# Convolution in blocks of 16 positions of one channel group, with tiles of one group of 16 rows

## The chip, the cores and the metric

The kernel runs on one core of one Trainium2 chip. The metric is the device time of one execution in microseconds (us). The core's engines are named as in the profile: PE (TensorE), DVE (VectorE), ACT (ScalarE), POOL (GpSimd) and SP (SyncE, which here only issues transfers). PE was granted a clock of 0.991 of full speed on average, which is its 2.4 GHz level almost throughout.

## What is computed

x is 128 x 32 x 512 (batch, channel, position), all float32. A grouped convolution over positions (4 groups of 8 channels, 9 taps, padding 4) plus a per-batch, per-channel condition is fed to a linear layer over the 512 positions with a routed LoRA; x is added to the result:

```python
out = lax.conv_general_dilated(x, weight, window_strides=(1,), padding=[(4, 4)],
        dimension_numbers=('NCH', 'OIH', 'NCH'), feature_group_count=4)
y = out + jnp.einsum('nd,od->no', c, c_weight)[:, :, None] + bias[None, :, None]
base_out = jnp.einsum('btd,od->bto', y, base_W) + base_b          # 512 -> 512
logits = jnp.einsum('btd,nd->btn', y, router_W) + router_b        # 512 -> 15
topk_p, topk_i = jax.lax.top_k(jax.nn.softmax(logits, -1), 8)
w = per-expert weight: topk_p summed by expert_map[topk_i]
h = jnp.einsum('btd,erd->bter', y, A)                             # 8 experts x 16
lora = jnp.einsum('bter,eor->bto', h * w[..., None], B) * 2.0
return x + base_out + lora
```

## The kernel before

Precision is kept by splitting each float32 operand into a high part (rounded by ACT) and a rest (the difference, made by DVE or POOL); every product is three matmuls: high by high, rest of the weights by high, high by rest of the data.

A tile is 128 rows of (batch, channel): 4 batches of 32 channels; there are 32 tiles, and the linear layer takes one tile per step. The convolution works in units of 16 channels (a half, h) of 8 batches, one unit per step, with blocks of 8 positions: partitions hold 8 positions x 16 channels. An output block needs two neighbouring input blocks. For even and odd blocks together this is done with three matrices: one for the block's own input, one for the reach into the next, and their sum. `terms` holds three operands of 256 columns: two differences of an even and an odd block (made by DVE, L672) and the odd block itself; so a unit is 3 x 3 = 9 matmuls of 256 columns (`conv`, L498). The sum of the shared product and the condition is made by DVE in `common` (L658), and added to both own products in one instruction of 512 columns that writes `y_rows` (L663). DVE turns `y_rows` into `y` by a block transposition (`turn`, L731), which needs both halves; ACT and POOL split it (`y_hi` L352, `y_lo` L443).

What an engine does in step t, in its own program order:
- PE (`step`): waits for `y_lo_ready` and `out_added`; 12 matmuls of 400 columns (the front bank: LoRA, router, half of the linear layer), then `front_done`; transposes `hw` of tile t-1 (`turn_hw`); 9 matmuls of 256; 6 of the LoRA's way up for tile t-1 (`up`, L540); 3 of 256; then `conv(t)`, which signals `common_done` after its first three matmuls and `conv_done` after the ninth.
- DVE: `condition` of the unit that PE made at the end of step t-1 (L658, L663), `turn(t+2)`, `difference` (L672 twice), `choose(t)` (L679, waits for `front_done`), `hw_low(t-1)`, `mark`, `weigh(t)` up to `hw` (L713), `add_out(t-1)` (L642, out of PSUM into `xr`), which signals `out_added`.
- ACT: `y_hi`, `hw_hi`, the exponentials, `terms_hi`, and a copy of the odd block to PSUM. POOL: `bias_rows` (L432), `y_lo`, `terms_lo` (L437). SP: stores and loads.

Steps 4 to 23 run in a loop of four steps each time round; 0 to 3 and 24 to 32 are written out. PSUM's two `wide_ps` sets alternate between tiles, so PE may begin step t only after `add_out(t-2)`, which is the last thing in DVE's step t-1. Before step 0 stands an opening that loads, splits and convolves the first tiles by ordinary products with two matrices; there POOL also adds the two convolution matrices (`conv_sum`).

## Time and profile before

| | |
|---|---|
| runs without the profiler | 197.27 us median of 3 (197.12, 197.27, 205.5) |
| the profiled execution's own time | 197.38 us |
| its span, first to last instruction | 195.6 us |
| busy: PE / DVE / POOL / ACT | 187.3 / 161.1 / 139.1 / 76.9 us |
| mean granted PE clock | 0.991 |
| bytes moved | 27.66 MB, 141 GB/s over the span |

The span is 1.8 us shorter than the time of the same execution. A row of the timeline gives the start and the duration; of DVE the duration of an instruction is longer than the distance to an independent next one. Matmuls are pipelined, so their durations overlap; the distance of two starts is what one costs on PE: 0.12 us for 256 columns, 0.18 us for 400. "idle before <-releaser" stands in brackets.

### The profile page before, as it was taken

To read this page: it belongs to the slowest core of one execution; us is meant where nothing else is said; L and a number is where in the kernel's file an instruction comes from. 1 tells how busy PE (TensorE), PEld (TensorE's weight loads), DVE (VectorE), ACT (ScalarE), POOL (GpSimd) and SP (SyncE) were. 2 spreads that over 40 slices of the span, in tenths; PEclk is the share of its full clock that TensorE was granted. 3 is DMA by queue.
4 is the path that set the end of the run, shared out by engine and by line. 5 is a ranking of instruction groups with operands and counts; after the bars stand their busy time and mean duration, and the time that the engine had idled before them with its cause. 6 is when DMAs were issued, how large, how long until landed. Compare 5 with 4: busy or idle time off the path is not lost.

```text
span 195.6 us, 4329 instructions
## 1 busy us (share of the span) xinstructions
PE 187.3 (96%) x1297; PEld 180.1 (92%) x1297; DVE 161.1 (82%) x547; ACT 76.9 (39%) x197; POOL 139.1 (71%) x115
## 2 busy tenths in 40 slices
PE   7899699999999999999999999999999999998993
PEld 2788599999999999999999999999999999997992
DVE  0899987888889888889888889888898889775663
ACT  3674434434333444433334444343344443122210
POOL 4539796777887777777887777778877777943520
PEclk9999969999999999999999999999999999999999
DMA  5985442455444434445443335444334133333312
GB/s 180 312 292 214 111 140 80 159 167 162 146 124 124 152 116 153 162 162 157 125 140 123 134 130 162 162 162 147 137 110 150 71 86 111 107 107 109 111 54 107
DMA packets 19051, 27.66 MB, mean 141 GB/s; under 512 B 2144, under 2 KB 9696, under 8 KB 19040
## 3 DMA queue, kind: packets, MB, share of 16 engines
q1 hardware_dynamic: 18576, 27.05, 42.6%
q10 hardware_dynamic: 432, 0.48, 0.7%
q8 instruction: 5, 0.08, 0.2%
q0 software_dynamic: 32, 0.01, 0.2%
q14 instruction: 6, 0.05, 0.1%
HBM read 19.14 MB, written 8.39 MB: 141 GB/s over the span
## 4 chain that ended last, share of the span: by engine, by line
PE 83%; DVE 8%; DMA 4%; issue 2%; ACT 1%; DVEq 0%; ACTq 0%
PE wide_ps L516 53%; PE conv_banks L498 15%; PE wide_ps L540 10%; DMA wide_sb<-wide_w 2%; DMA x_in<-x_first 2%; PE hwt_bank L527 2%; PE conv_banks L516 1%; DVE terms L672 1%; DVE y_rows L647 1%; DVE xr L642 1%; DVE wide_lo L757 1%; DVE y L731 1%; DVE spread L703 0%; DVE expert_w L707 0%; ACT wide_hi L324 0%
## 5 line engine op out<-in xcount | busy, mean ns | idle before, releaser
L516 PE MATMUL wide_ps<-wide_hi,y_hi 128*128 128x400 f32 (+1 forms) x248 | 80.4, 329 | 1.1 <-DVE xr L642 0.8
L516 PE MATMUL wide_ps<-wide_lo,y_hi 128*128 128x400 f32 (+1 forms) x248 | 77.1, 315 | 0.0
L516 PE MATMUL wide_ps<-wide_hi,y_lo 128*128 128x400 f32 (+1 forms) x248 | 76.8, 314 | 0.0
L437 POOL TENSOR_TENSOR terms_lo<-terms,terms_hi 128x768 fp32r<-128x768 f32 x28 | 51.6, 1842 | 31.8 <-ACT terms_hi L345 31.8
L516 PEld LDWEIGHTS wide_ps<-wide_hi,y_hi 128*128 128x128 f32 x248 | 46.6, 189 | 3.5 <-issue 1.0
L516 PEld LDWEIGHTS wide_ps<-wide_lo,y_hi 128*128 128x128 f32 x248 | 46.9, 190 | 0.0
L516 PEld LDWEIGHTS wide_ps<-wide_hi,y_lo 128*128 128x128 f32 x248 | 46.6, 189 | 0.0
L432 POOL TENSOR_TENSOR xr<-xr,biases_sb 128x512 f32<-128x512 f32 x32 | 41.3, 1291 | 5.6 <-DMA xr<-x_rows 5.5
L443 POOL TENSOR_TENSOR y_lo<-y,y_hi 128x512 fp32r<-128x512 f32 x31 | 40.2, 1295 | 3.3 <-ACT y_hi L352 3.3
L359 ACT ACTIVATE hw_hi<-hwt_bank 128x128 fp32r<-128x128 f32 x31 | 8.6, 277 | 81.7 <-PE hwt_bank L527 81.7
L352 ACT ACTIVATE y_hi<-y 128x512 fp32r<-128x512 f32 x32 | 20.2, 632 | 17.9 <-PE wide_ps L516 16.8
L345 ACT ACTIVATE terms_hi<-terms 128x768 fp32r<-128x768 f32 x28 | 23.2, 830 | 2.5 <-DVE terms L672 2.5
L498 PE MATMUL conv_banks<-terms_lo,conv_hi 128*128 128x256 f32 x84 | 24.0, 286 | 0.0
L498 PE MATMUL conv_banks<-terms_hi,conv_lo 128*128 128x256 f32 x84 | 24.0, 285 | 0.0
L498 PE MATMUL conv_banks<-terms_hi,conv_hi 128*128 128x256 f32 x84 | 23.9, 285 | 0.0
L731 DVE STREAM_TRANSPOSE y<-y_rows 128x512 f32<-128x512 f32 x32 | 22.6, 707 | 1.0
L663 DVE TENSOR_TENSOR y_rows<-conv_banks,common 128x512 f32<-128x512 f32 x28 | 19.4, 692 | 2.9
L642 DVE TENSOR_TENSOR xr<-wide_ps,xr 128x512 f32<-128x512 f32 x30 | 20.4, 682 | 0.5 <-PE wide_ps L540 0.3
L672 DVE TENSOR_TENSOR terms<-even,odd_bank 128x256 f32<-128x256 f32 x56 | 20.0, 395 | 0.0
L498 PEld LDWEIGHTS conv_banks<-terms_hi,conv_hi 128*128 128x128 f32 x84 | 16.0, 191 | 0.3 <-issue 0.3
L498 PEld LDWEIGHTS conv_banks<-terms_hi,conv_lo 128*128 128x128 f32 x84 | 16.1, 192 | 0.0
L498 PEld LDWEIGHTS conv_banks<-terms_lo,conv_hi 128*128 128x128 f32 x84 | 16.1, 191 | 0.0
...
## 6 DMA issues: line engine op xcount, KB each, us to landing
...
```

The lines of the kernel that those rows point to most:

```text
L345: nc.scalar.activation(terms_hi[i % 2][:, :, :, :], terms[i][:, :, :, :], ACT.Copy)\
L352: nc.scalar.activation(y_hi[k % 2][:, :, :], y[k % 2][:, :, :], ACT.Copy)\
L432: nc.gpsimd.tensor_tensor(xr[k][:, :], xr[k][:, :], base_b_sb[:, :], ALU.add)\
L437: nc.gpsimd.tensor_tensor(terms_lo[i % 2][:, :, :, :], terms[i][:, :, :, :], terms_hi[i % 2][:, :, :, :].bitcast(F32), ALU.subtract)\
L443: nc.gpsimd.tensor_tensor(y_lo[k % 2][:, :, :], y[k % 2][:, :, :], y_hi[k % 2][:, :, :].bitcast(F32), ALU.subtract)\
L498: mm = nc.tensor.matmul(sums, w[:, h, j, :], a[i][:, j, :, :], start=w is conv_hi and a is terms_hi, stop=a is terms_lo)
L516: mm = nc.tensor.matmul(sums_of(t, k)[:, b, 0:columns[1] - columns[0]], a[k % 2][:, r, :], w[:, r, columns[0]:columns[1]], start=r == 0 an ...
L540: mm = nc.tensor.matmul(sums_of(t, k)[:, b, first:first + HALF], a[k % 2][:, :], w[:, b * HALF:(b + 1) * HALF], start=False, stop=True, sk ...
L642: nc.vector.tensor_tensor(rows, linear_sums(t, k), rows, ALU.add)\
L663: nc.vector.tensor_tensor(y_rows[i][:, h, :, :].rearrange("p n (a k) -> p a n k", a=2), own_ps, common[:, :, :].unsqueeze(1).to_broadcast( ...
L672: d = nc.vector.tensor_tensor(terms[i][:, j, :, :], even[i][:, :, j:j + MK], odd_ps, ALU.subtract)
L731: nc.vector.transpose(y[k % 2][:, :, :].rearrange("p r (n h o) -> p h n r o", n=Q, h=HALVES), y_rows[(k // 2) % 2][:, :, own, :]).then_inc ...
```

## The change

Partitions now hold 16 positions x 8 channels: a unit is one channel group (of 4) of 16 batches, and a tile of the linear layer is that same unit, 128 rows of (batch, channel of the group). The input is brought into this order on the host (`x_units`, `x_edges`, `x_rows`), and the output back from it.

In blocks of 16 positions, an output block reaches into its neighbour with 8 positions only, half of the partitions; groups of even number reach forward, those of odd number backward, so that their reaching halves are different partitions. The products of the unit with its own and its sum matrix are 2 x 3 = 6 matmuls of 256 columns; the edges of two groups lie in one operand and one matrix (`edges`, `W_QUARTERS`, `edge_ps` in `hwt_bank`), 3 matmuls, made with the group of even number. So `conv` has 9 matmuls in odd steps and 6 in even steps. There is one difference per unit on DVE instead of two, and on POOL one edge difference and one `edge_lo` per two tiles; ACT has one `edge_hi` per two tiles; `terms_hi` and `terms_lo` have 512 columns instead of 768.

`condition` now waits for `conv_done` ahead of its first instruction, and has three instructions of 256 columns, each of which waits for the one before: shared product plus condition, own product plus that, and the edge product on 64 partitions. `turn(t)` needs only its own unit. `turn_hw(t-1)` of step t also waits until `condition(t+2)` is done, since the edge product is in the bank of its output. Fourteen matrices are loaded instead of four, in five pieces, and `conv_sum` is gone. In the opening the condition's weights and `expert_map` are loaded from ACT's queue behind the table load, POOL's `map_f` stands behind the splitting of the second matrix piece and the second input tile, and DVE makes `is_expert` in eight instructions ahead of the first `y_rows` rather than in one behind `turn(1)`. `add_out(0)` and `hw_low(0)` move within DVE's steps 0 and 1.

```diff
+CG = C // GROUPS
+BP = P // CG
+Q = P // CG
+TILES = N * C // P
+BLK = L // BP
+BLKI = BLK + 1
+MK = BLK // 2
+EDGE = P // 2
+START = 4
+RUNS = BP // 4
...
+W_OWN, W_REACH = (0, 2, 4, 6), (1, 3, 5, 7)
+W_SUM, W_QUARTERS = (8, 9, 11, 12), (10, 13)
+W_ALL = 14
+W_PIECES = (slice(0, 2), slice(2, 4), slice(4, 8), slice(8, 11), slice(11, 14))
...
-            act.dma_start(conv_sb[:, :, :, :], conv_w).then_inc(conv_w_in, 16)
-            act.dma_start(cond_in_sb[:, :], cond).then_inc(cond_in, 16)
+            for piece in range(2):
+                own = W_PIECES[piece]
+                act.dma_start(conv_sb[:, own, :], conv_w[:, own, :]).then_inc(conv_w_in[piece], 16)
             act.wait_ge(zeros_ready, 1)
             nc.scalar.activation(zero_exp[:, :], zeros[:, 0:1], ACT.Exp)
-            act.wait_ge(conv_w_in, 16)
-            for h in range(HALVES):
-                nc.scalar.activation(conv_hi[:, h, 0:BLOCKS, :], conv_sb[:, h, :, :], ACT.Copy)\
+            act.dma_start(cond_in_sb[:, :], cond).then_inc(cond_in, 16)
+            act.dma_start(map_i[:, :], expert_map.partition_broadcast(P)).then_inc(map_in, 16)
...
+                cond_w_in_sb.unsqueeze(2).to_broadcast([P, GROUPS, BP, CG])).then_inc(cond_w_ready, 1)
+
+            def conv_low_later(piece):
+                pool.wait_ge(conv_hi_ready, piece + 1)
+                conv_low(nc.gpsimd, piece, conv_lo_ready)
+
+            def x_low_later(i):
+                pool.wait_ge(x_hi_ready, i + 1)
+                x_low(nc.gpsimd, i, x_lo_ready)
+
+            conv_low_later(1)
+            x_low_later(1)
             pool.wait_ge(map_in, 16)
             nc.gpsimd.tensor_copy(map_f[:, :], map_i[:, :]).then_inc(map_ready, 1)
...
+            conv_low_later(2)
+            x_low_later(2)
+            x_low_later(3)
...
+            def conv(t, g, p):
+
+                h = g % 2
+                pe.wait_ge(terms_lo_ready, t - START + 1)
+                parts = [(conv_ps[:, h, 0, :, :], W_SUM[g], terms_hi[h][:, 1], terms_lo[h][:, 1]),
+                         (conv_ps[:, h, 1, :, :], W_OWN[g], terms_hi[h][:, 0], terms_lo[h][:, 0])]
                 if h == 0:
...
+                    pe.wait_ge(y_rows_ready, t)
+                    parts.append((edge_ps, W_QUARTERS[g // 2], edge_hi, edge_lo))
+                else:
+                    pe.wait_ge(y_rows_ready, t - 1)
+                if isinstance(t, int) and t < 2 * START and h == 0:
+                    pe.wait_ge(conv_lo_ready, 3 + g // 2)
+                for n, (sums, j, hi, lo) in enumerate(parts):
+                    if n == 2:
+                        pe.wait_ge(edge_lo_ready, p - START // 2 + 1)
+                    for w, a in ((conv_hi, hi), (conv_lo, hi), (conv_hi, lo)):
+                        mm = nc.tensor.matmul(sums, w[:, j, :], a[:, :, :],
+                                              start=w is conv_hi and a is hi, stop=a is lo)
                 mm.then_inc(conv_done, 1)
...
             def turn_hw(t, k):
+                if from_tile(t, 1) and up_to_tile(t, TILES - 4):
+
+                    pe.wait_ge(y_rows_ready, t + 4)
...
-                if from_tile(t, 1) and up_to_tile(t, TILES - 5):
-                    conv(t, k, p)
+                if from_tile(t, 1) and up_to_tile(t, TILES - 4):
+                    conv(t + 3, (k + 3) % GROUPS, p + 2)
 
...
-            def add_condition(rows, sums, c, ready):
-                batches = c.shape[1]
+            def condition_first(t):
+                dve.wait_ge(conv_done, t + 1)
+                c = cond_sb[:, t, 0:Q]
                 nc.vector.tensor_tensor(
...
+                    y_rows[t % 2][:, :, :, :],
+                    first_ps[:, t % 2, :, :].rearrange("p n (k a) -> p n a k", a=2),
+                    c.unsqueeze(2).unsqueeze(3).to_broadcast([P, Q, 2, MK]), ALU.add)\
+                    .then_inc(y_rows_ready, 1)
+
+            def condition(t, g, q):
+
+
+
+                h = g % 2
+                shared, other = 1 - h, h
+                rows = y_rows[h]
+                reached = slice(EDGE, P) if h == 0 else slice(0, EDGE)
+                dve.wait_ge(conv_done, t + 1)
+                c = cond_sb[:, g, bass.ds(q * Q, Q)]
+                nc.vector.tensor_tensor(rows[:, :, shared, :], conv_ps[:, h, 0, :, :],
+                                        c.unsqueeze(2).to_broadcast([P, Q, MK]), ALU.add)\
                     .then_inc(common_ready, 1)
...
+                dve.wait_ge(common_ready, t - START + 1)
+                nc.vector.tensor_tensor(rows[:, :, other, :], conv_ps[:, h, 1, :, :],
+                                        rows[:, :, shared, :], ALU.add).then_inc(own_ready, 1)
+                dve.wait_ge(own_ready, t - START + 1)
+                nc.vector.tensor_tensor(rows[reached, :, shared, :], edge_ps[reached],
+                                        rows[reached, :, shared, :], ALU.add)\
                     .then_inc(y_rows_ready, 1)
 
...
+            def difference(t, i):
+
+                dve.wait_ge(odd_ready, t - START + 1)
+                nc.vector.tensor_tensor(terms[i][:, 0, :, :], terms[i][:, 0, :, :], odd_ps,
+                                        ALU.subtract).then_inc(differences_ready, 1)
...
             wide_low(0)
-            dve.wait_ge(cond_summed, 1)
-            nc.vector.tensor_tensor(cond_sb[:, :, :], cond_ps,
-                                    conv_b_sb.unsqueeze(2).to_broadcast([P, HALVES, N]), ALU.add)\
-                .then_inc(cond_biased, 1)
-            dve.wait_ge(cond_biased, 1)
-            first_rows(0, first_ps)
+            dve.wait_ge(map_ready, 1)
+            for e in range(E):
+                nc.vector.tensor_scalar(is_expert[:, e, :], map_f[:, :], float(e), None,
+                                        ALU.is_equal).then_inc(is_expert_ready, 1)
+            bias_condition(0)
+            condition_first(0)
+            turn(0, 0)
...
-            first_rows(1, conv_ps[:, :, Q:, :])
-            dve.wait_ge(map_ready, 1)
-            dve.wait_ge(ids_ready, E)
-            nc.vector.tensor_tensor(is_expert[:, :, :],
-                                    map_f[:, :].unsqueeze(1).to_broadcast([P, E, ROUTES]),
-                                    expert_ids[:, :].unsqueeze(2).to_broadcast([P, E, ROUTES]),
-                                    ALU.is_equal).then_inc(is_expert_ready, 1)
-            difference(FIRST_UNIT, 0)
+            condition_first(1)
+            turn(1, 1)
+            bias_condition(1)
+            difference(START, 0)
...
+            def step(t, k, p, q):
+                if isinstance(t, int) and t < START - 2:
+                    condition_first(t + 2)
+                elif up_to_tile(t, TILES - 3):
+                    condition(t + 2, (k + 2) % GROUPS, q + (k + 2) // GROUPS)
                 if up_to_tile(t, TILES - 3):
                     turn(t + 2, k + 2)
-                if up_to_tile(t, TILES - 6):
-                    difference(t + 5, (k + 1) % URING)
```

DVE at the beginning of its step 2, before the change (`conv_done` and `common_done` are PE's signals, the other waits but `front_done`, `odd_ready` and `y_lo_ready` are on DVE itself):

```order
L658 TENSOR_TENSOR common<-conv_banks,cond_sb 128x256 [waits common_done]
L663 TENSOR_TENSOR y_rows<-conv_banks,common 128x2x8x32 [waits common_ready,conv_done]
L731 STREAM_TRANSPOSE y<-y_rows 128x2x4x4x16 [waits y_lo_ready,y_rows_ready]
L672 TENSOR_TENSOR terms<-even,odd_bank 128x256 [waits odd_ready]
L672 TENSOR_TENSOR terms<-even,odd_bank 128x256
L679 TENSOR_TENSOR logits<-wide_ps,biases_sb 128x15 [waits front_done]
```

and after it:

```order
L745 TENSOR_TENSOR y_rows<-conv_banks,cond_sb 128x16x16 [waits conv_done]
L749 TENSOR_TENSOR y_rows<-conv_banks,y_rows 128x16x16 [waits common_ready]
L752 TENSOR_TENSOR y_rows<-hwt_bank,y_rows 64x16x16 [waits own_ready]
L812 STREAM_TRANSPOSE y<-y_rows 128x16x4x8 [waits y_lo_ready,y_rows_ready]
L759 TENSOR_TENSOR terms<-terms,odd_bank 128x256 [waits odd_ready]
L765 TENSOR_TENSOR logits<-wide_ps,biases_sb 128x15 [waits front_done]
```

The first instruction now waits for the whole convolution rather than for its first third, three instructions stand in the place of two, and one difference in the place of two.

PE at the end of step 1 and the beginning of step 2 (the last six of the nine matmuls of `conv`, then the next tile's first), before:

```order
L498 MATMUL conv_banks<-terms_hi,conv_hi 128x256
L498 MATMUL conv_banks<-terms_hi,conv_lo 128x256
L498 MATMUL conv_banks<-terms_lo,conv_hi 128x256
L498 MATMUL conv_banks<-terms_hi,conv_hi 128x256
L498 MATMUL conv_banks<-terms_hi,conv_lo 128x256
L498 MATMUL conv_banks<-terms_lo,conv_hi 128x256
L516 MATMUL wide_ps<-wide_hi,y_hi 128x400 [waits out_added,y_lo_ready]
L516 MATMUL wide_ps<-wide_lo,y_hi 128x400
```

and after:

```order
L579 MATMUL conv_banks<-terms_hi,conv_hi 128x256
L579 MATMUL conv_banks<-terms_hi,conv_lo 128x256
L579 MATMUL conv_banks<-terms_lo,conv_hi 128x256
L579 MATMUL hwt_bank<-edge_hi,conv_hi 128x256 [waits edge_lo_ready]
L579 MATMUL hwt_bank<-edge_hi,conv_lo 128x256
L579 MATMUL hwt_bank<-edge_lo,conv_hi 128x256
L593 MATMUL wide_ps<-wide_hi,y_hi 128x400 [waits out_added,y_lo_ready]
L593 MATMUL wide_ps<-wide_lo,y_hi 128x400
```

The last three matmuls of the unit are the edges; in the next step (2) the six remain and these three are missing.

POOL in the opening, before:

```order
L413 MEMSET expert_ids 128x1 x8
L415 COPY cond_w_sb<-cond_in_sb 128x256 [waits cond_in]
L224 TENSOR_TENSOR x_lo<-x_in,x_hi 128x260 [waits x_hi_ready]
L224 TENSOR_TENSOR x_lo<-x_in,x_hi 128x260
L422 CAST map_f<-map_i 128x15 [waits map_in]
L424 TENSOR_TENSOR conv_sum<-conv_sb 128x256 [waits conv_w_in]
```

and after:

```order
L455 COPY cond_w_sb<-cond_in_sb 128x512 [waits cond_in]
L228 TENSOR_TENSOR conv_lo<-conv_sb,conv_hi 128x256 [waits conv_hi_ready]
L223 TENSOR_TENSOR x_lo<-x_in,x_hi 128x528 [waits x_hi_ready]
L470 CAST map_f<-map_i 128x15 [waits map_in]
L228 TENSOR_TENSOR conv_lo<-conv_sb,conv_hi 128x512 [waits conv_hi_ready]
```

Behind the wait for `cond_in` the split of a matrix piece is new, and `map_f` is behind it and behind `x_lo` of tile 1; in DVE's new order the rows after `wide_lo` are:

```order
L835 TENSOR_TENSOR wide_lo<-wide_sb,wide_hi 128x656 [waits wide_hi_ready]
L851 TENSOR_SCALAR is_expert<-map_f 128x15 [waits map_ready]
L851 TENSOR_SCALAR is_expert<-map_f 128x15 x7
L842 TENSOR_TENSOR cond_sb<-hwt_bank,cond_in_sb 128x256 [waits cond_summed]
L729 TENSOR_TENSOR y_rows<-conv_banks,cond_sb 128x512 [waits conv_done,cond_biased]
L812 STREAM_TRANSPOSE y<-y_rows 128x16x4x8 [waits y_rows_ready]
```

So the first `y_rows` of the program now stands behind `map_ready`, POOL's signal of `map_f`; before, `is_expert` stood behind the second `turn`.

## Rows read from the trace of the kernel before

**Rows 1.** The page: busy us (share of the span) of each engine; the chain by line.
```profile
PE 187.3 (96%) x1297; PEld 180.1 (92%) x1297; DVE 161.1 (82%) x547; ACT 76.9 (39%) x197; POOL 139.1 (71%) x115
...
PE wide_ps L516 53%; PE conv_banks L498 15%; PE wide_ps L540 10%; DMA wide_sb<-wide_w 2%; DMA x_in<-x_first 2%; PE hwt_bank L527 2%; PE conv_banks L516 1%; DVE terms L672 1%; DVE y_rows L647 1%; DVE xr L642 1%; DVE wide_lo L757 1%; DVE y L731 1%; DVE spread L703 0%; DVE expert_w L707 0%; ACT wide_hi L324 0%
```

**Rows 2.** Stretches: start:end, length, busy us (instructions) by engine, clock, DMA share, GB/s.
```profile
33.56:172.11 138.55, 138.55 (x1003) 137.11 (x1001) 122.17 (x424) 55.74 (x147) 108.49 (x77) 1.00 0.42 136
172.11:177.59 5.48, 4.63 (x34) 4.42 (x32) 4.27 (x16) 1.27 (x4) 2.54 (x3) 1.00 0.30 96
...
25.00:29.00 4.00, 4.00 (x20) 3.88 (x19) 3.52 (x8) 1.24 (x3) 4.00 (x3) 0.58 0.44 134
```

**Rows 3.** The chain in order of time, one tile step: start us, us, what.
```profile
105.79 2.19 PE wide_ps L516 x12
...
110.22 1.06 PE conv_banks L498 x9
```

**Rows 4.** Timeline of PE: start us, us, engine, line, op, out<-in, count.
```profile
105.50 0.29 PE L498 MATMUL conv_banks<-terms_lo,conv_hi 128*128 128x256 f32 x1
105.62 0.34 PE L516 MATMUL wide_ps<-wide_hi,y_hi 128*128 128x400 f32 x1
...
111.01 0.28 PE L498 MATMUL conv_banks<-terms_lo,conv_hi 128*128 128x256 f32 x1
111.18 0.42 PE L516 MATMUL wide_ps<-wide_hi,y_hi 128*128 128x400 f32 x1
111.44 0.34 PE L516 MATMUL wide_ps<-wide_lo,y_hi 128*128 128x400 f32 x1
```

**Rows 5.** Timeline of DVE over the same tile step and the one before.
```profile
102.50 0.17 DVE L679 TENSOR_TENSOR logits<-wide_ps,biases_sb 128x15 f32<-128x15 f32 x1 [0.22 <-PE wide_ps L516]
...
104.73 0.68 DVE L642 TENSOR_TENSOR xr<-wide_ps,xr 128x512 f32<-128x512 f32 x1
105.33 0.41 DVE L658 TENSOR_TENSOR common<-conv_banks,cond_sb 128x256 f32<-128x256 f32 x1
105.85 0.69 DVE L663 TENSOR_TENSOR y_rows<-conv_banks,common 128x512 f32<-128x512 f32 x1
106.67 0.71 DVE L731 STREAM_TRANSPOSE y<-y_rows 128x512 f32<-128x512 f32 x1
107.30 0.71 DVE L672 TENSOR_TENSOR terms<-even,odd_bank 128x256 f32<-128x256 f32 x2
108.02 0.17 DVE L679 TENSOR_TENSOR logits<-wide_ps,biases_sb 128x15 f32<-128x15 f32 x1
...
110.35 0.68 DVE L642 TENSOR_TENSOR xr<-wide_ps,xr 128x512 f32<-128x512 f32 x1
```

**Rows 6.** Groups by shape: busy us, mean ns of one, idle time before them.
```profile
L672 DVE TENSOR_TENSOR terms<-even,odd_bank 128x256 f32<-128x256 f32 x56 | 20.0, 395 | 0.0
...
L658 DVE TENSOR_TENSOR common<-conv_banks,cond_sb 128x256 f32<-128x256 f32 x28 | 11.6, 415 | 0.0
```

**Rows 7.** The opening, timelines of ACT, POOL and DVE.
```profile
2.96 0.20 ACT L311 ACTIVATE zero_exp<-zeros 128x1 f32<-128x1 bf16 x1
5.88 0.40 POOL L415 COPY cond_w_sb<-cond_in_sb 128x256 f32<-128x256 f32 x1 [2.69 <-DMA cond_in_sb<-cond]
8.91 0.20 POOL L422 CAST map_f<-map_i 128x15 f32<-128x15 int32 x1
...
14.26 1.25 DVE L786 TENSOR_TENSOR is_expert<-map_f,expert_ids 128x120 f32<-128x120 f32 x1
```

**Rows 8.** The opening: POOL by shape, one DMA, ACT before PE and PE after DVE.
```profile
L224 POOL TENSOR_TENSOR x_lo<-x_in,x_hi 128x520 fp32r<-128x520 f32 x2 | 2.6, 1336 | 2.9 <-ACT x_hi L318 2.9
...
cond_in_sb<-cond ACTq DMA_DIRECT2D x1, 81.0 KB, 4.6
...
10.75 1.47 PE L516 MATMUL wide_ps<-wide_hi,y_hi 128*128 128x400 f32 x8 [0.23 <-ACT y_hi L352]
...
24.65 0.50 PE L540 MATMUL wide_ps<-up_hi,hw_lo 128*128 128x256 f32 x2 [1.01 <-DVE hw_lo L742]
```

501 lines of the change are left out of this document (249 added, 252 removed).

## Prediction

> **What bounds the kernel now.** I read the page first: PE is busy 96% of the span and DVE 82%, and the chain that ended last runs almost wholly through PE [rows 1]. That says "PE", but a busy share doesn't say how near the second engine is. So next the stretches: from 33.56 to 172.11 us there are 25 tile steps in 138.55 us, 5.54 each, PE busy throughout at full clock; in the step from 172.11 to 177.59, in which PE has no convolution, the step still takes 5.48 although PE works 4.63 of it [rows 2]. Nine matmuls fewer, and 0.06 us won: something just behind PE has a period of its own.
>
> The two timelines show it [rows 4, 5]. PE begins a tile at S = 105.62. DVE takes up the logits of that tile at 108.02, which is S + 2.40 and as soon as the twelve front matmuls allow (2.19 in the chain [rows 3]); then 2.33 to the start of `add_out` at 110.35, 0.68 for it, and PE begins the next tile at 111.18, 0.15 later. PE's last convolution matmul started at 111.01, and matmuls of 256 columns stand 0.118 apart (1.06 / 9 [rows 3]), so PE was ready at 111.13 and waited 0.05 for `out_added`. In the step before, logits to `add_out` took 2.23 (102.50 to 104.73). The ring front bank, logits, `hw`, `add_out`, next front bank is thus 2.40 + 2.23 + 0.69 + 0.15 = 5.47 (5.57 in the first of the loop's four steps, where DVE takes 0.10 more), against 5.51 of PE's own work (5.56 less the wait). Two engines are critical at once, with 0.04 between them. The reader is to see that a saving on PE is worth nothing by itself, and a delay on DVE ahead of the logits counts from 0.04 on.
>
> **PE's part.** Removed: 1.5 matmuls of 256 columns a unit, 28 units, 0.118 each: 5.0 us [rows 3]. All of it falls in even steps, which have 6 convolution matmuls: PE's own work there is 5.51 - 0.35 = 5.16. Odd steps keep 9 and 5.51. By the ring, a saving in even steps can show only down to 5.47.
>
> **DVE's part.** Before, `common` started while PE was still convolving (105.33, that is S - 0.29), the 512 instruction at 105.85, `turn` 0.82 later, the two differences 0.63 later (0.71 together), logits at S + 2.40 [rows 5]. Now the first instruction waits for `conv_done`. The 512 instruction, which waited for the same signal, started at S + 0.23, and the last matmul's row ends at 105.79, S + 0.17 [rows 4, 5]; I take 0.22. Then three dependent instructions. `common` takes 0.41, and the one that depends on it starts 0.52 after its start [rows 5]; on PSUM and SBUF operands of 256 columns an instruction takes 0.395 to 0.415 [rows 6], and I take the same for the one on 64 partitions, since its columns are the same (no row has fewer partitions; at half the price it would save 0.2). So 0.52 + 0.52, and 0.54 to `turn` (0.41, and 0.13 as from the 512 instruction to `turn`: 0.82 - 0.69); `turn` to the difference 0.63; one difference to the next instruction 0.32 (0.71 less 0.395).
>
> Where the step before had 9 matmuls, PE starts this tile at once, S is the end of the convolution, and the logits start at S + 0.22 + 0.52 + 0.52 + 0.54 + 0.63 + 0.32 = S + 2.75, 0.35 later than now. Nothing behind them gets shorter, since up to `hw` DVE waits for itself: 2.75 + 2.23 + 0.69 + 0.15 = 5.82 to the next S, 5.92 in the loop's first step. This is an even step, with 5.16 of work for PE, which then stands 0.66. What is late next: PE's next front bank; `turn_hw`, which now also waits for `condition`, has it at S + 1.8 and is itself due at S + 2.2, so that wait is free.
>
> In the odd step that follows, the convolution has been done 0.4 before `add_out` ends, DVE starts `condition` at S - 0.23 (0.60 after the start of `add_out`, as 104.73 to 105.33), and the front bank ends last again. After a wait PE's first matmul takes 0.26 instead of 0.18 (111.18 to 111.44 [rows 4]), so the step is 5.51 + 0.08 = 5.59, and the ring 5.55.
>
> The sum over steps 3 to 28 (33.56 to 177.59, 144.03 before [rows 2]): 13 odd steps of 5.59 = 72.7; 13 even, 5 of them of 5.92 and 8 of 5.82 = 76.2. Together 148.9, **+4.9 us**.
>
> **POOL, ACT, DMA.** POOL per tile: 256 columns less of `terms_lo`, 256 more of edges; ACT about the same. Both have a tile step of 5.5 with 4.35 and 2.2 busy (108.49 and 55.74 over 25 [rows 2]), which hides it; without that cover it would be some 0.2 a tile. Loads of the convolution grow from two to three operands of 256 columns a tile, at a DMA share of 0.42 [rows 2]; hidden, since nothing in the steady part waits for a transfer.
>
> **The opening.** The condition's load was issued at 1.19 and took 4.6 [rows 8]; now it stands behind the table load and the first exponential, which ends at 3.16 [rows 7], so it lands near 7.8 (5.8 if it is only 2.6 under way). POOL waits for it, copies twice the columns (0.7 for 0.40), splits matrix piece 1 (0.74) and `x_lo` of 528 (1.34 [rows 8]), then `map_f` 0.2: 10.8, instead of 8.91 + 0.20. DVE waits for that ahead of its first `y_rows`: eight small instructions 0.7, then 0.43 + 0.69 + 0.71 and 0.6 of ACT, 0.3 between them: PE's step 0 starts at 14.2 instead of 10.75 [rows 8]. Much is won back: DVE no longer has `is_expert` of 1.25 behind `turn(1)` [rows 7], and the wait of PE for `hw_lo` at 24.65 [rows 8] comes at 24.3. But the logits of step 1 are 3.0 later (26.8), and `turn_hw` of step 2 must wait for `condition(4)` behind them. Followed through in this way step 3 starts at 34.8 instead of 33.56, at 33.1 if the condition lands at 5.8. Another spell at half clock like that of 25 to 29 us (0.58 [rows 2]) would cost up to 1.6. I take **+1.0**, from -0.5 to +2.5. The end, after step 28, has no convolution, and I take 0.
>
> **Sum.** 195.6 + 4.9 + 1.0 = 201.5 of span; with the 1.8 around it 203.3, against 197.38 for the profiled execution. The median is 0.1 less than that one: **203.2 us**, +3.0%.
>
> **Bounds.** Downward: dependent DVE instructions at their bare 0.415, 0.415 and 0.415, 0.71 and 0.395 behind them: 2.57 instead of 2.75, which is 13 x 0.18 = 2.3 less; with the opening at -0.5, 199.4. Upward: another 0.13 for each of `conv_done` and the first dependent instruction, 3.4, which with the opening at +2.5 would be 208; I don't let both ends meet and stop at 207.
>
> The Trainium skill, "VectorE: DVE Perf Modes", section "The DRAIN you can't avoid", says that a semaphore between two Vector instructions costs nothing extra, as the next one can't start before the pipe is empty anyway. By that rule the sum would be the downward one, 200.9 with the opening at +1.0. The trace speaks against it: 0.52 from a `common` of 0.41, but 0.60 from an `add_out` of 0.68 to an instruction that doesn't need its result [rows 5].
>
> **Rivals.**
> - Slower by the chain from `conv_done` to the logits, as above: 203.2, own range 201 to 207, chance 0.66.
> - The wait costs nothing and dependent instructions follow at their bare duration, as in the bound: 200.9, within 2%, chance 0.12. For it: the gap of 0.11 is from one form of instruction. Against: it stands in each of the 28 units.
> - The DVE chain is not later at all, for instance because the edge instruction takes half; then the ring holds even steps at 5.47 to 5.57 and PE odd ones at 5.51 to 5.59: no change in the steady part, 198.3 with the opening, chance 0.10.
> - Faster: the saving on PE arrives. It would need `add_out` to be off PE's path in even steps; then 5.0 less and the opening 1.0 more, 193.3. The rows at 111.01 and 111.18, and the step without a convolution at 5.48 [rows 2], speak against it: it decides itself at a ring under 5.16. Chance 0.08, an opening that gets faster by its smaller first matrix load included.
> - PE's clock falls in the pauses of 0.66: each spell like that at 25 to 29 us costs 1.6; 205 to 210. Against: in the step that holds a pause of 0.85 (5.48 less 4.63) the clock is 1.00 [rows 2]. Chance 0.04.
>
> By more than 2%, about what a measurement of this kernel can tell from no change (3.9 us): slower 0.66 + 0.04, less the lowest edge, 0.68; within 0.24; faster 0.08. The range, 199.0 (a little under the lower bound) to 207, leaves out the faster case and the one without change.
>
> **What would show it.** `add_out`'s end and PE's next front bank 0.15 apart in every step; PE idle some 0.6 a pair of tiles, put down to `xr`; steps alternating near 5.85 and 5.6; logits at S + 2.75 in even steps, S + 2.5 in odd; the first DVE instruction of `condition` waiting for PE in even steps alone. Wrong would be: logits near S + 2.4 in even steps, even steps under 5.5, or step 3 beginning well off 34.5.

## The result and the profile after

The changed kernel takes 201.75 us (201.65 to 201.89), the kernel before 197.19: ratio 1.0248, 95% interval 1.0212 to 1.0283, so it is slower by 2.5%. (The ratios leave out executions that ran slow, one of the kernel before with 205.5 and one of the kernel before with its `add_out` early with 197.4; the medians don't.) The profiled executions differ by less, 201.71 against 197.38 (spans of 199.6 and 195.6): the kernel before varies from 196.2 to 198.7 between executions, and the one profiled is not one of its shortest.

The page after, beside [rows 1]: PE's busy time has fallen by 3.1 us, its share to 92%, and only 44% of the last chain now runs through PE, with 36% through DVE.

```profile
span 199.6 us, 4275 instructions
...
PE 184.2 (92%) x1246; PEld 173.5 (87%) x1246; DVE 160.7 (81%) x551; ACT 76.8 (38%) x214; POOL 145.3 (73%) x135
...
PE 44%; DVE 36%; POOL 7%; issue 6%; DMA 2%; DVEq 1%; ACT 1%; ACTq 0%
```

The list of waits after (us in total, times, longest): PE waits 14 times for `xr`, and DVE 13 times for the last edge matmul.

```profile
PE wide_ps L593 <- DVE xr L723: 6.7, 14, 0.6
...
DVE y_rows L745 <- PE hwt_bank L579: 6.1, 13, 0.5
```

The stretches after, beside [rows 2] (columns as there): up to step 3, the steps 3 to 27, step 28, and the rest.

```profile
0.00:33.60 33.60, 27.83 (x146) 20.99 (x146) 24.29 (x68) 17.25 (x38) 23.55 (x28) 1.00 0.68 228
33.60:176.02 142.42, 136.45 (x965) 133.22 (x965) 120.98 (x425) 55.37 (x161) 113.21 (x102) 1.00 0.49 153
176.02:181.52 5.50, 5.35 (x40) 5.13 (x38) 4.70 (x17) 1.28 (x4) 3.46 (x4) 1.00 0.30 95
181.52:199.60 18.08, 14.63 (x100) 14.12 (x100) 10.68 (x43) 2.88 (x11) 5.11 (x4) 1.00 0.32 103
```

Step 3 begins at 33.60 (33.56 before), steps 3 to 28 take 147.92 instead of 144.03, and what follows takes 18.08 instead of 18.01. The whole of the difference between the traces, +3.9, is in the steady part; it lies in the even steps.

PE's timeline after: the end of a convolution of nine matmuls, the start S = 107.81 of an even step, and the start of the next one, 5.97 later. The matching rows of before are [rows 4].

```profile
107.33 0.28 PE L579 MATMUL conv_banks<-terms_lo,conv_hi 128*128 128x256 f32 x1
107.45 0.29 PE L579 MATMUL hwt_bank<-edge_hi,conv_hi 128*128 128x256 f32 x1
...
107.69 0.28 PE L579 MATMUL hwt_bank<-edge_lo,conv_hi 128*128 128x256 f32 x1
107.81 0.34 PE L593 MATMUL wide_ps<-wide_hi,y_hi 128*128 128x400 f32 x1
...
113.78 0.42 PE L593 MATMUL wide_ps<-wide_hi,y_hi 128*128 128x400 f32 x1 [0.59 <-DVE xr L723]
```

DVE's timeline of that step, and the first instructions of the next (before: [rows 5]):

```profile
108.12 0.42 DVE L745 TENSOR_TENSOR y_rows<-conv_banks,cond_sb 128x256 f32<-128x256 f32 x1 [0.48 <-PE hwt_bank L579]
108.58 0.42 DVE L749 TENSOR_TENSOR y_rows<-conv_banks,y_rows 128x256 f32<-128x256 f32 x1
109.04 0.43 DVE L752 TENSOR_TENSOR y_rows<-hwt_bank,y_rows 64x256 f32<-64x256 f32 x1
109.59 0.71 DVE L812 STREAM_TRANSPOSE y<-y_rows 128x512 f32<-128x512 f32 x1
110.34 0.42 DVE L759 TENSOR_TENSOR terms<-terms,odd_bank 128x256 f32<-128x256 f32 x1
110.68 0.17 DVE L765 TENSOR_TENSOR logits<-wide_ps,biases_sb 128x15 f32<-128x15 f32 x1
...
112.95 0.68 DVE L723 TENSOR_TENSOR xr<-wide_ps,xr 128x512 f32<-128x512 f32 x1
113.55 0.41 DVE L745 TENSOR_TENSOR y_rows<-conv_banks,cond_sb 128x256 f32<-128x256 f32 x1
...
115.00 0.71 DVE L812 STREAM_TRANSPOSE y<-y_rows 128x512 f32<-128x512 f32 x1
115.63 0.38 DVE L759 TENSOR_TENSOR terms<-terms,odd_bank 128x256 f32<-128x256 f32 x1
116.24 0.17 DVE L765 TENSOR_TENSOR logits<-wide_ps,biases_sb 128x15 f32<-128x15 f32 x1 [0.23 <-PE wide_ps L593]
```

In the even step the logits start at S + 2.87, straight behind the difference and with no wait for the front bank; in the odd step (S = 113.78) at S + 2.46, behind a wait for it. `add_out` ends at 113.63 and PE goes on 0.15 later. In the loop of four steps, k is the number of the step in the loop, from 0 to 3. Even steps take 5.97 or 5.98 where k is 0, 5.79 or 5.80 where k is 2, and 5.67 in the written-out steps 24 and 26; odd steps take 5.54 to 5.58.

### The profile page after: what moved, and what is told of

Its sections match the earlier page's. It is cut to its first block, busy times and chain, and to the rows that moved or that the text cites. A ratio compares the mean times of both kernels' runs of the same rounds, so it can differ in the third digit from the quotient of the medians.

```text
span 199.6 us, 4275 instructions
## 1 busy us (share of the span) xinstructions
PE 184.2 (92%) x1246; PEld 173.5 (87%) x1246; DVE 160.7 (81%) x551; ACT 76.8 (38%) x214; POOL 145.3 (73%) x135
## 4 chain that ended last, share of the span: by engine, by line
PE 44%; DVE 36%; POOL 7%; issue 6%; DMA 2%; DVEq 1%; ACT 1%; ACTq 0%
PE wide_ps L593 29%; DVE xr L723 6%; PE wide_ps L627 5%; DVE y L812 5%; PE conv_banks L579 5%; DVE terms L759 3%; DVE y_rows L752 3%; DVE y_rows L749 3%; DVE y_rows L745 3%; DMA cond_in_sb<-cond 2%; PE hwt_bank L579 2%; DVE spread L789 2%; DVE expert_w L793 2%; POOL x_lo L223 2%; DVE hw_lo L824 2%
## 5 line engine op out<-in xcount | busy, mean ns | idle before, releaser
L482 POOL TENSOR_TENSOR terms_lo<-terms,terms_hi 128x512 fp32r<-128x512 f32 x28 | 36.2, 1294 | 29.2 <-ACT terms_hi L374 29.1
L374 ACT ACTIVATE terms_hi<-terms 128x512 fp32r<-128x512 f32 x28 | 17.2, 616 | 0.0
L745 DVE TENSOR_TENSOR y_rows<-conv_banks,cond_sb 128x256 f32<-128x256 f32 x28 | 11.8, 420 | 6.1 <-PE hwt_bank L579 6.1
L579 PE MATMUL conv_banks<-terms_hi,conv_lo 128*128 128x256 f32 x56 | 15.8, 282 | 0.0
L579 PE MATMUL conv_banks<-terms_hi,conv_hi 128*128 128x256 f32 x56 | 15.7, 281 | 0.0
L579 PE MATMUL conv_banks<-terms_lo,conv_hi 128*128 128x256 f32 x56 | 15.7, 280 | 0.0
L799 DVE SCALAR_TENSOR_TENSOR hw<-wide_ps,inv,expert_w 128x128 f32<-128x128 f32 x31 | 10.9, 351 | 4.4
L359 ACT ACTIVATE exps<-logits,minus_best 128x15 f32<-128x15 f32 x32 | 9.8, 308 | 11.4 <-DVE minus_best L768 11.4
L627 PE MATMUL wide_ps<-up_hi,hw_lo 128*128 128x256 f32 x62 | 13.0, 289 | 0.0
L749 DVE TENSOR_TENSOR y_rows<-conv_banks,y_rows 128x256 f32<-128x256 f32 x28 | 11.9, 425 | 1.0
```

The lines of the kernel that those rows point to most:

```text
L374: nc.scalar.activation(terms_hi[i % 2][:, :, :, :], terms[i][:, :, :, :], ACT.Copy)\
L482: nc.gpsimd.tensor_tensor(terms_lo[i % 2][:, :, :, :], terms[i][:, :, :, :], terms_hi[i % 2][:, :, :, :].bitcast(F32), ALU.subtract)\
L579: mm = nc.tensor.matmul(sums, w[:, j, :], a[:, :, :], start=w is conv_hi and a is hi, stop=a is lo)
L627: mm = nc.tensor.matmul(sums_of(t, k)[:, b, first:first + HALF], a[k % 2][:, :], w[:, b * HALF:(b + 1) * HALF], start=False, stop=True, sk ...
L745: nc.vector.tensor_tensor(rows[:, :, shared, :], conv_ps[:, h, 0, :, :], c.unsqueeze(2).to_broadcast([P, Q, MK]), ALU.add)\
L749: nc.vector.tensor_tensor(rows[:, :, other, :], conv_ps[:, h, 1, :, :], rows[:, :, shared, :], ALU.add).then_inc(own_ready, 1)
```

## The experiments

There are two theories, and a third for some of the runs. The ring is the loop front bank, logits, `hw`, `add_out`, next front bank. **Wait**: the way from the last convolution matmul through `condition` to the logits, joined to the rest of the ring, makes the even steps, and PE's saving can't arrive. **Work**: DVE's added instructions make the steps longer wherever they stand. **PE**: PE's own matmuls or inputs set the steps. All runs were compared with the kernel before on their chip, whose median was 197.15, 197.85, 196.65 and 197.44 in the four groups. "Steady part" is the time from the start of step 3 to that of step 29.

### PE's saving alone, in the kernel before

```diff
-                for j in (TERMS - 1, 0, 1):
+                for j in (TERMS - 1, 0) + ((1,) if k % 2 else ()):
```

> The kernel before, with the second own product left out in units of even number: 6 convolution matmuls instead of 9 in 13 or 14 of 28 units, so part of the convolution isn't computed. It measures what PE's saving is worth alone. Theory 'ring' (front bank, logits, hw, add_out, next front bank have a period of 5.47 to 5.57 of their own): even steps stay at 5.47 to 5.57, the whole at 196.5 to 197.2 us, PE idle by 0.3 in even steps with add_out's xr as the releaser. Rival 'PE' (PE sets the steps and its saving arrives): 13 x 3 x 0.118 = 4.6 less, 192.6 us.

Measured: 197.61 against 197.15, ratio 1.0002 (0.997 to 1.0035). PE's timeline, the last of six matmuls and the next step:

```profile
122.33 0.28 PE L498 MATMUL conv_banks<-terms_lo,conv_hi 128*128 128x256 f32 x1
122.76 0.42 PE L516 MATMUL wide_ps<-wide_hi,y_hi 128*128 128x400 f32 x1
```

The next front bank starts 0.43 after the last convolution matmul instead of 0.12. The steady part is 144.15 (144.03 before): 36 matmuls less, in its 12 even steps with a convolution, are worth nothing. The even steps went to 5.46 to 5.56, and the odd ones behind their waits to 5.57 to 5.61. That is the ring, and the theory that PE sets the steps falls.

### The late wait alone, in the kernel before

```diff
-                dve.wait_ge(common_done, t)
+                dve.wait_ge(conv_done, t + 2)
```

> The kernel before, with one wait changed: DVE's `common` waits for the unit's ninth matmul instead of its third. Same instructions, same result. Theory 'wait': logits at S + 0.22 + 0.52 + 0.82 + 0.63 + 0.71 = S + 2.90 instead of 2.40 where PE starts a tile right behind the convolution; such a step takes 5.97 (6.07 in the first of four), and in the step behind it the convolution is done before add_out ends, which makes it 5.56 to 5.59: steps alternate although all have nine matmuls; 13 pairs of 11.55 to 11.6 instead of 11.08: 203.3 us. Rival 'work': DVE does what it did before, so no change, 197.2. Rival 'not later' (front bank ends last anyway): under 1 us more.

Measured: 200.92 against 197.15, ratio 1.0206 (1.0149 to 1.0262). The steady part is 148.09, +4.06, where the whole change brought +3.9. DVE's timeline, in which S is 107.19 and the next step starts at 113.18:

```profile
107.54 0.42 DVE L658 TENSOR_TENSOR common<-conv_banks,cond_sb 128x256 f32<-128x256 f32 x1 [0.55 <-PE conv_banks L498]
108.00 0.69 DVE L662 TENSOR_TENSOR y_rows<-conv_banks,common 128x512 f32<-128x512 f32 x1
108.82 0.71 DVE L730 STREAM_TRANSPOSE y<-y_rows 128x512 f32<-128x512 f32 x1
109.45 0.71 DVE L671 TENSOR_TENSOR terms<-even,odd_bank 128x256 f32<-128x256 f32 x2
110.09 0.16 DVE L678 TENSOR_TENSOR logits<-wide_ps,biases_sb 128x15 f32<-128x15 f32 x1
```

One wait is later and no instruction is added: steps of 5.94 to 6.01 (k is 0), 5.78 (k is 2) and 5.66 (24 and 26) alternate with steps of 5.57 or 5.58 (one of 5.63), although every unit has nine matmuls, and the long ones are the even ones here too. The alternation comes from the ring itself: behind a long step PE has finished the convolution before `add_out` ends. The expected total was 2.4 too high: 2.0 of that is in the steady part (+6.1 expected), and step 3 began at 32.89 instead of 33.56. `common` to the 512 instruction is 0.46, not 0.52, of which more below.

### The wait taken back, in the changed kernel

PE gives a signal of its own after the sixth matmul (the two sums and the edges are in different banks):

```diff
+                    if h == 0 and n == 1:
+                        mm.then_inc(sums_done, 1)
...
-                dve.wait_ge(conv_done, t + 1)
+                if h == 0:
+                    dve.wait_ge(sums_done, p)
+                else:
+                    dve.wait_ge(conv_done, t + 1)
```

The edge instruction waits for `conv_done` in its place.

> The changed kernel, but in units with nine matmuls PE signals also after the sixth (both sums), and DVE's first two instructions of `condition` wait for that, only the edge instruction for the ninth. Nothing is left out; DVE has the same work. Theory 'wait' (the prediction's: the way from conv_done through three dependent instructions to the logits sets even steps): the first instruction moves 3 x 0.118 = 0.35 earlier in 13 even steps, from S + 0.20/0.32 to S - 0.15/-0.03; even steps 5.97 and 5.80 become about 5.62 and 5.45; 13 x 0.35 = 4.6 less: 197.2 us. Rival 'work' (the steps are longer because DVE's instructions take more time, wherever they stand): no change, 201.7. Rival 'PE' (the steps are set by PE's own inputs, y_lo): no change or under 1 us.

Measured: 198.68 against 197.15, ratio 1.0077 (1.0052 to 1.0101); steady part 144.91, 3.0 less than the changed kernel's 147.92, where 4.6 was expected. DVE's timeline at S = 106.29:

```profile
106.26 0.42 DVE L751 TENSOR_TENSOR y_rows<-conv_banks,cond_sb 128x256 f32<-128x256 f32 x1 [0.15 <-PE conv_banks L580]
106.72 0.42 DVE L755 TENSOR_TENSOR y_rows<-conv_banks,y_rows 128x256 f32<-128x256 f32 x1
107.27 0.43 DVE L760 TENSOR_TENSOR y_rows<-hwt_bank,y_rows 64x256 f32<-64x256 f32 x1
```

The first instruction is 0.35 earlier, as expected. The edge instruction, which now has two waits, starts 0.55 after the one before it instead of 0.46, so the logits come at S + 2.61 and not 2.52, and the step is 5.71. That is so only in the loop: in step 24, which is written out, the same instruction with the same two waits starts 0.46 after the one before (151.73 behind 151.27). Where k is 2 they are at 2.52 and the step is 5.53; in steps 24 and 26 the front bank ends last again and the last part of the 0.35 is lost. The work is the same and the time is 3.0 us less, so "work" falls.

### Other work put into the wait

```diff
+                if from_tile(t, 2) and up_to_tile(t, TILES - 5):
+                    difference(t + 4, k)
                 if isinstance(t, int) and t < START - 2:
                     condition_first(t + 2)
...
-                if up_to_tile(t, TILES - 5):
+                if not from_tile(t, 2):
                     difference(t + 4, k)
```

> The changed kernel with `difference` ahead of `condition` in DVE's steps from 2 on, instead of behind `turn`: it then runs in the 0.5 us in which DVE waits for conv_done in even steps. Nothing is left out. Theory 'wait': logits 0.33 earlier in even steps, which become 5.64 and 5.47; odd steps stay at 5.56, since the front bank ends last there; 13 x 0.33 = 4.3 less: 197.4 us; the held 0.11 between turn and difference goes as well if the difference no longer stands behind an instruction on partitions 64 to 127. Rival 'work': no change, 201.7. If the operand's copy by ACT comes late (odd_ready), DVE would wait for it: 201 to 203.

Measured: 197.80 against 197.15, ratio 1.003 (1.0014 to 1.0046); steady part 144.04. DVE's timeline at S = 105.56:

```profile
105.31 0.41 DVE L759 TENSOR_TENSOR terms<-terms,odd_bank 128x256 f32<-128x256 f32 x1
105.88 0.42 DVE L745 TENSOR_TENSOR y_rows<-conv_banks,cond_sb 128x256 f32<-128x256 f32 x1 [0.16 <-PE hwt_bank L579]
...
107.26 0.71 DVE L812 STREAM_TRANSPOSE y<-y_rows 128x512 f32<-128x512 f32 x1
108.00 0.17 DVE L765 TENSOR_TENSOR logits<-wide_ps,biases_sb 128x15 f32<-128x15 f32 x1
```

`condition` starts at S + 0.32 as before, but nothing stands between `turn` and the logits, which start at S + 2.44 (2.42 to 2.49 over the even steps). All that the change had lost in the steady part is won back by the order of DVE's program. The 0.11 by which the difference was late behind `turn` (0.74 instead of 0.63) was expected to go and didn't; it moved to the logits (`turn` to logits 0.74).

### The start partition of the edge instruction

```diff
-                reached = slice(EDGE, P) if h == 0 else slice(0, EDGE)
+                reached = slice(0, EDGE)
```

> The changed kernel, in which DVE's edge instruction works on partitions 0 to 63 for all groups, instead of 64 to 127 for the even ones, so that half of the edges of even groups go to the wrong rows; the same number of instructions and elements. In the changed kernel turn to difference takes 0.63 in odd steps and 0.74 in even ones, where the edge instruction in front of turn reads PSUM from partition 64. The trace says 'held instruction': if it is the start partition, all steps have 0.63, even steps are 0.11 shorter, 13 x 0.11 = 1.4 less: 200.3 us. The Trainium skill, VectorE: DVE Perf Modes, section 'Two Vector instructions with no wait between them', has the rule that an instruction whose input starts in another quadrant than the last one read from that memory waits until all earlier ones are finished. Rival 'parity' (even steps are late for another reason, such as what POOL or ACT do there): 0.74 stays, 201.7 us.

Measured: 199.68 against 197.85, ratio 1.0116 (1.0071 to 1.0161); steady part 145.93, 2.0 less than the changed kernel. DVE's timeline in an even step:

```profile
107.88 0.42 DVE L752 TENSOR_TENSOR y_rows<-hwt_bank,y_rows 64x256 f32<-64x256 f32 x1
108.42 0.71 DVE L812 STREAM_TRANSPOSE y<-y_rows 128x512 f32<-128x512 f32 x1
109.06 0.38 DVE L759 TENSOR_TENSOR terms<-terms,odd_bank 128x256 f32<-128x256 f32 x1
109.36 0.16 DVE L765 TENSOR_TENSOR logits<-wide_ps,biases_sb 128x15 f32<-128x15 f32 x1
```

`turn` to difference is 0.63 or 0.64 in every step. From the difference to the logits it is now 0.30 instead of 0.34, which I had not counted (1.4 us expected in all, 2.0 measured): together 0.15 for each even step. The edit moved all three operands of the edge instruction, in PSUM and in SBUF. `turn`, which stands between it and the difference, reads and writes SBUF alone, from partition 0; so what the difference meets is the start in PSUM. That step is argued; no run moved the PSUM operand alone.

### The other end of the ring

`add_out(t-1)` goes ahead of the instruction that writes `hw` of tile t: in the changed kernel, then in the kernel before with six matmuls in even units, and with nine. The diff is that of the changed kernel; in the kernel before, `from_tile(t, 1)` stands for `from_tile(t, 2)` in it:

```diff
+                if between:
+                    between()
                 if from_tile(t, 2):
                     dve.wait_ge(hwt_done, t - 1)
...
-                    weigh(t, k)
-                if from_tile(t, 2) and up_to_tile(t, TILES - 3):
-                    add_out(t - 1, (k - 1) % UNROLL)
+                    adds = from_tile(t, 2) and up_to_tile(t, TILES - 3)
+                    weigh(t, k, (lambda: add_out(t - 1, (k - 1) % UNROLL)) if adds else None)
```

> The changed kernel with `add_out(t-1)` ahead of the instruction that writes `hw` of tile t, instead of behind it; nothing is left out. PE starts its next tile only after add_out. Theory 'ring' (the even steps are as long as front bank, condition, logits, add_out make them, and PE's saving is hidden by that ring): logits to add_out falls from 2.23 by the 0.38 that hw takes to about 1.85, as far as the LoRA's way up on PE is done by then (S + 4.4); even steps 5.97 and 5.80 become about 5.6 and 5.45, odd ones stay at PE's 5.51 to 5.56; 13 x 0.36 = 4.7 less: 197.1 us. Rival 'hw' (the next tile waits for hw through turn_hw, so what add_out gains hw loses): 201.7.

> The kernel before with six instead of nine convolution matmuls in units of even number (part of the convolution isn't computed) and add_out ahead of hw. The first edit alone was worth nothing (197.61 beside 197.15). Theory 'ring': with the ring shortened by 0.38 PE's saving arrives, as far as the LoRA's way up allows: even steps 5.28 to 5.35, odd ones PE's 5.51 to 5.58, a pair of 10.85 instead of 11.08; 13 x 0.23 = 3.0 less than 197.6: 194.6 us. Rival 'PE's matmuls are not what it could save' (another wait takes the place): 197.6.

> The kernel before with add_out ahead of hw and all nine matmuls; nothing is left out. It tells what the convolution in blocks of 16 is worth once the ring is shorter: the changed kernel with its three edits took 192.83. Theory 'ring and PE are two bounds': the ring is now 5.18, PE's own 5.51 to 5.52 sets every step; only the waits of 0.05 go: 26 x 0.02 to 0.05 = 0.5 to 1.3 less, 196.0 to 196.7 us, so that PE's saving of 4.6 is worth 3.5 to 4. Rival 'the order of DVE is all of it': 193 to 194, as the changed kernel with the edits.

Measured: the changed kernel with this edit 195.13 against 197.85, ratio 0.988 (0.9839 to 0.9921). The kernel before with six matmuls in even units 192.62, ratio 0.9756 (0.9708 to 0.9804); with nine 194.60 against 196.65, ratio 0.9878 (0.9831 to 0.9926). The steady parts are 141.68, 140.05 and 142.77. The first two came out 2.0 under what was expected: 1.5 and 1.1 of that are in the steady part, where more than 0.38 was won, and the rest is in the opening.

In the changed kernel logits to `add_out` fell from 2.27 and 2.18 to 1.77 and 1.69, 0.5 and not 0.38, because `add_out` also needn't wait for the end of the reduction that `hw` depends on; it starts 0.20 behind its start (DVE's timeline):

```profile
108.86 0.28 DVE L793 TENSOR_REDUCE expert_w<-spread 128x8 f32<-128x120 f32 x1
109.06 0.68 DVE L723 TENSOR_TENSOR xr<-wide_ps,xr 128x512 f32<-128x512 f32 x1
109.66 0.34 DVE L801 SCALAR_TENSOR_TENSOR hw<-wide_ps,inv,expert_w 128x128 f32<-128x128 f32 x1
```

The pair of runs with six and nine matmuls is the clearest evidence on PE: the same 36 matmuls, worth nothing while the ring stood at 5.47 to 5.57, are worth 142.77 - 140.05 = 2.7 us once it stands at 5.19. With nine matmuls every step with a convolution is PE's own 5.50 or 5.51; step 28, which has none, takes the ring's 5.19. The total of 194.60 is 1.4 below what I expected: the steady part gave the 1.26 expected at most, and step 3 began at 32.20.

### The three edits together, and what the change is then worth

> The changed kernel with the three edits together: a signal after the sixth matmul, `difference` ahead of `condition`, `add_out` ahead of hw; nothing is left out. Theory 'ring': in even steps logits follow the front bank (S + 2.42), add_out can start at S + 4.3 to 4.45 (behind logits by 1.85, and behind the LoRA's way up), so the step is 4.4 + 0.68 + 0.15 = 5.25 to 5.35; odd steps have PE's own 5.51 to 5.59; a pair of 10.85 where `difference` ahead alone has 144.04 / 13 = 11.08: 3.0 less than its 197.8, 194.8 us, and faster than the kernel before by 1.2%. Rival 'other bound' (POOL or ACT, or turn_hw waiting for hw, holds a pair at 11.08): 197.8.

Measured: 192.83 against 197.85, ratio 0.9756 (0.9715 to 0.9797), faster than both kernels, and 2.0 under what was expected. In the steady part PE has no idle time left that the stretches show:

```profile
33.23:167.50 134.27, 134.27 (x964) 132.51 (x965) 120.57 (x427) 55.04 (x161) 113.87 (x102) 1.00 0.52 163
167.50:172.68 5.18, 5.18 (x39) 5.08 (x38) 4.32 (x16) 1.14 (x4) 3.45 (x3) 1.00 0.29 101
```

Even steps take 5.15 to 5.18, odd ones 5.54 to 5.57, together 139.45. This isn't quite PE alone: at the end of each even step the next front bank starts 0.14 or 0.15 behind the end of `add_out` and 0.16 behind the last matmul instead of 0.12, and its first matmul takes 0.42 as after a wait, so the ring still ends about 0.04 behind PE there. Against the kernel before with its `add_out` early (142.77), the convolution in blocks of 16 saves 3.3 us in the steady part. There it has 30 matmuls of 256 columns less, 3.5 us at 0.118 each, since its step 28 has six and that of the kernel before none. In these two executions 1.0 of it is lost in the opening (step 3 at 33.23 against 32.20), which varies, as said below; the medians are 192.83 and 194.60, 1.8 apart and taken on different chips. The change was held back by the order around it.

### The opening

One run puts `is_expert` behind `turn(1)`, as in the kernel before; another puts `map_f` sooner on POOL. Both have the three edits:

```diff
-            dve.wait_ge(map_ready, 1)
-            for e in range(E):
-                nc.vector.tensor_scalar(is_expert[:, e, :], map_f[:, :], float(e), None, ...
...
             turn(1, 1)
+            dve.wait_ge(map_ready, 1)
+            for e in range(E):
+                nc.vector.tensor_scalar(is_expert[:, e, :], map_f[:, :], float(e), None, ...
```

```diff
-            x_low_later(1)
             pool.wait_ge(map_in, 16)
             nc.gpsimd.tensor_copy(map_f[:, :], map_i[:, :]).then_inc(map_ready, 1)
+            x_low_later(1)
```

> The changed kernel with the three edits, and is_expert's eight instructions behind turn(1) again, as in the kernel before, instead of ahead of the first y_rows; nothing is left out. DVE waited 2.63 us for map_f there and PE's step 0 started at 12.8 instead of 10.75. Theory 'the opening's chain goes through map_f': first y_rows at 8.7 instead of 10.6, step 0 at 10.9; POOL, which is busy without a gap from 13.96 on because conv_hi stands behind y_hi on ACT, starts up to 1.9 earlier too, and step 3 comes 1.0 to 1.9 earlier: 191 to 191.9 us. Rival 'later waits set step 3' (DVE's logits of step 1, the matrices' loads, POOL's string of instructions): step 0 earlier, step 3 within 0.3 of 33.2, 192.8 us.

> The changed kernel with the three edits, and POOL's `map_f` one instruction sooner, ahead of the splitting of the second input tile (1.34 us) instead of behind it; nothing is left out. is_expert was worse off when it stood behind turn(1): its eight instructions took 3.40 us beside POOL's instructions instead of 0.71, and the whole took 193.82 instead of 192.83. Here it stays where POOL leaves DVE alone. Theory 'a chain through map_f sets step 0, and step 0 passes on what it gains when nothing is put in its place': map_f at 8.1, is_expert at 8.3, step 0 at 11.6 instead of 12.9, POOL's long string of instructions from 12.8 instead of 14.0, step 3 at 32.0 to 32.5 instead of 33.23: 191.6 to 192.1 us. Rival 'step 3 is set by loads and by POOL's string whatever step 0 does': within 0.3 of 192.8. Rival 'clock': waits of PE of 0.9 to 1.2 us between 22 and 25 us are followed by a stretch at 0.58 of full clock, as in the kernel before and in the last run: 193 to 194.5.

Measured: 193.82 (ratio 0.9852, 0.9815 to 0.9889) and 193.07 (0.98, 0.9754 to 0.9847), so neither beats 192.83, and both missed what was expected (191 to 191.9 and 191.6 to 192.1). In the first, step 0 began 1.5 earlier, at 11.37, and step 3 later, at 34.50. In the second nothing moved (12.80, 33.12). The rows of DVE's timelines say why; the eight small instructions are one row. In the changed kernel without the three edits, with POOL idle from 9.51 to 13.96:

```profile
9.55 0.71 DVE L851 TENSOR_SCALAR is_expert<-map_f 128x15 f32<-128x15 f32 x8 [2.63 <-POOL map_f L470]
```

In the first run, DVE and then POOL beside it:

```profile
15.92 3.40 DVE L873 TENSOR_SCALAR is_expert<-map_f 128x15 f32<-128x15 f32 x8
```

```profile
13.91 3.19 POOL L224 TENSOR_TENSOR x_lo<-x_in,x_hi 128x528 fp32r<-128x528 f32 x2
17.07 1.29 POOL L501 TENSOR_TENSOR y_lo<-y,y_hi 128x512 fp32r<-128x512 f32 x1
```

In the second run, DVE and then POOL beside it:

```profile
8.47 1.81 DVE L861 TENSOR_SCALAR is_expert<-map_f 128x15 f32<-128x15 f32 x8 [1.42 <-POOL map_f L470]
```

```profile
8.39 1.34 POOL L224 TENSOR_TENSOR x_lo<-x_in,x_hi 128x528 fp32r<-128x528 f32 x1
```

With POOL idle the eight take 0.71. Beside one of POOL's splittings they take 1.81 and end where they ended before; beside POOL's instructions in a row they take 3.40. That POOL is what slows them is read from these placements; no run changed POOL's work beside them and nothing else. In the second run the wait was only exchanged for slowness. In the first, the profiled execution also has the stretch at a granted clock of 0.58 from 25 to 29 us, behind waits of PE of 1.23 at 22.41 and 0.92 at 24.68, as in the kernel before [rows 2]:

```profile
25.00:29.00 4.00, 4.00 (x22) 4.00 (x21) 3.40 (x13) 1.16 (x5) 4.00 (x5) 0.58 0.71 199
```

Such waits don't settle it by themselves: PE waited 0.74 and 1.00 at 23.20 and 24.92 in the kernel before with `add_out` early, and 1.12 and 1.01 at 24.27 and 25.99 in the one with six matmuls, and from 25 to 29 us both were granted 1.00.

The stretch accounts for little of the result: executions with a mean clock of 0.998 to 1.0 took 193.68 to 193.86, against 194.19 for the profiled one with 0.991. How much of the later step 3 is the 3.40 and how much the other waits wasn't separated.

## Why the prediction was right

**Forecast 203.2, measured 201.75**, slower by the mechanism named; the even steps carry it. The 1.45 between them are 1.0 too much for the steady part and 1.0 too much for the opening, less 0.3 for the time around the span, which was 2.1 and not 1.8; the rest is rounding and the 0.1 between a profiled execution and the median.

- *The ring, 0.04 behind PE.* Right. Six matmuls for nine moved the steady part by +0.12.
- *PE's saving of 5.0 worthless.* Right. It arrives as far as the ring is shortened: 1.1 of it with `add_out` early alone (142.77 to 141.68), 3.3 with all three edits. Of the 5.0, the steady part holds 3.5 (30 matmuls); I had not counted the six matmuls that step 28 gains.
- *0.63 from `turn` to the difference.* Right in odd steps; 0.74 in even ones, and 0.04 more behind it, for which I had no term. That this, the 0.32 and the gaps read too long nearly cancelled is luck: logits at S + 2.87, 2.78 and 2.66 against my 2.75.
- *Even steps 5.92 and 5.82.* Measured 5.97, 5.80, 5.67 (steps 24, 26), and 5.50 for step 28, which I had counted as a long one: DVE has no difference there, and the front bank ends last. The 13 sum to 75.7, not 76.2.
- *Odd steps 5.59.* Measured 5.54 to 5.58, 72.2 in all instead of 72.7. With the above the steady part is +3.9 instead of +4.9.
- *The opening +1.0.* +0.04 in the two profiles. The condition's load landed by 6.77, where POOL's copy of it starts (below), not at 7.8: it was issued at 1.73 by ACT's timeline, and not behind the exponential that stands ahead of it in the program and ended at 3.16. It took 5.0 from issue to landing. Step 0 came at 12.77, not 14.2. But the +0.04 sets a step 3 with no stretch at half clock against one with it [rows 2]. The four runs with the old opening and no such stretch began step 3 at 32.20, 32.82, 32.89 and 33.92, and their step 0 between 11.02 and 12.09; beside them the 33.60 is 1.4 later to 0.3 sooner. What the new opening costs is within my range and not settled: +1.0 is neither borne out nor refuted.
- *POOL, ACT, loads, `turn_hw`'s new wait, the tail: nothing.* Right; the tail changed by 0.07.

POOL's timeline after, and the transfer (KB, us from issue to landing):

```profile
6.77 0.62 POOL L455 COPY cond_w_sb<-cond_in_sb 128x512 f32<-128x512 f32 x1 [4.82 <-DMA cond_in_sb<-cond]
```

```profile
cond_in_sb<-cond ACTq DMA_DIRECT2D x1, 82.0 KB, 5.0
```

The rival with bare durations, 200.9, is nearer to the measured 201.75 than my 203.2. Its gaps were nearly right (0.46 is nearer to 0.415 than to 0.52), but by it the logits would come at S + 2.57, and they came at 2.66 to 2.87, by the wait in the loop and the late difference, which neither sum had. "Not later at all" fell with the edge instruction: 0.42 on 64 partitions, as on 128. "Faster" fell with the wait of PE for `xr`, 6.7 us. The granted clock was 1.00 over the steady part, through all pauses of 0.6.
